# Spread weight rows and a straight scale product in a blockwise FP4 feed-forward kernel

## The reference

```python
def fp4_quant_dequant(x):            # BLOCK = 16, along the last dim
    xb = x.reshape(shape[:-1] + (shape[-1] // BLOCK, BLOCK))
    scale = jnp.max(jnp.abs(xb), axis=-1, keepdims=True) / 6.0
    scale = jnp.maximum(scale, jnp.float32(1e-12))
    xn = xb / scale
    idx = jnp.searchsorted(_MID, jnp.abs(xn))
    q = _GRID[idx] * jnp.sign(xn) * scale
    return q.reshape(shape)

def fp4_linear(x, w):
    return jnp.einsum('bsk,nk->bsn', fp4_quant_dequant(x), fp4_quant_dequant(w))

gate = fp4_linear(x, w_gate)
y = fp4_linear(x, w_up)
h = jax.nn.silu(gate) * y            # 1408 wide, quantised again inside the next line
return fp4_linear(h, w_down)
```

## Time and profile before

| | us |
|---|---|
| median of three runs | 1740.33 |
| lowest, highest | 1736.83, 1742.61 |
| the profiled execution | 1740.98 |
| its span in the profile | 1739.2 |
| TensorE busy | 1482.2 |
| ScalarE busy | 1347.2 |
| VectorE busy | 1169.9 |

### The profile page before, as it was taken

How to read it: one execution, slowest core, us unless ns; L and a number is a source line. 1 busy time by engine, 2 the same in 40 slices (tenths; PEclk the granted TensorE clock), 3 DMA queues, 4 the chain that set the end, 5 groups by cost and what they waited for, 6 DMA issues and landing times.

```text
span 1739.2 us, 23935 instructions
## 1 busy us (share of the span) xinstructions
PE 1482.2 (85%) x9752; PEld 651.5 (37%) x9752; DVE 1169.9 (67%) x2111; ACT 1347.2 (77%) x1391; POOL 2.7 (0%) x18
## 2 busy tenths in 40 slices
PE   6788888765888899889999999899999998689886
PEld 4234444311333333333333333333333334345442
DVE  4579999864475435467655555676555557999994
ACT  2798898899999999969999999699999992000000
POOL 0000000000000000000000000000000000000000
PEclk9999999888999999999999999999999999899997
DMA  3123332330011111211211111102211111122212
GB/s 129 37 62 75 74 75 63 76 73 15 13 24 35 35 35 24 36 35 16 55 36 36 36 36 35 36 13 59 35 36 36 35 36 36 37 54 62 58 41 51
DMA packets 180754, 77.88 MB, mean 45 GB/s; under 512 B 163851, under 2 KB 163851, under 8 KB 180645
## 3 DMA queue, kind: packets, MB, share of 16 engines
q1 hardware_dynamic: 177392, 74.99, 19.0%
q10 hardware_dynamic: 3253, 1.37, 0.3%
HBM read 27.85 MB, written 8.39 MB: 21 GB/s over the span
## 4 chain that ended last, share of the span: by engine, by line
ACT 56%; DVE 29%; PE 11%; issue 2%; ACTq 1%; DMA 1%; DVEq 0%; SPq 0%
ACT hring L438 54%; DVE work L703 4%; PE rho L548 3%; DVE work L714 2%; DVE work L715 2%; DVE sm L694 2%; ACT th L458 2%; DVE work L909 1%; DVE work L908 1%; DVE sm L697 1%; DVE work L713 1%; DVE work L712 1%; PE dn L623 1%; DVE work L716 1%; DVE work L717 1%
## 5 line engine op out<-in xcount | busy, mean ns | idle before, releaser
L438 ACT ACTIVATE hring<-featT,bias 128x1024 f32<-128x1024 f32 x1232 | 1293.0, 1140 | 80.9 <-PE rho L548 76.2
L548 PE MATMUL rho<-hring,wslide 128*32 128x512 f32 x4928 | 614.9, 623 | 136.7 <-ACT hring L438 136.7
L548 PEld LDWEIGHTS rho<-hring,wslide 128*32 128x32 f32 x4928 | 133.5, 112 | 499.9 <-ACT hring L438 271.7
L623 PE MATMUL dn<-wd_room,turned 128*128 128x512 f16 x1056 | 243.7, 383 | 13.4 <-DMA turned<-work 13.4
L908 DVE SCALAR_TENSOR_TENSOR work<-th,gu1g 128x352 f32<-128x352 f32 x64 | 33.3, 521 | 266.6 <-ACT th L458 265.9
L611 PE MATMUL gu0g<-wg,turned 128*128 128x352 f16 x768 | 134.6, 328 | 45.8 <-DVE work L909 29.0
L623 PEld LDWEIGHTS dn<-wd_room,turned 128*128 128x128 f16 x1056 | 99.2, 98 | 175.2 <-issue 54.6
L458 ACT ACTIVATE th<-gu0g 128x352 f32<-128x352 f32 x64 | 28.9, 451 | 171.5 <-PE gu0u L611 171.5
L611 PE MATMUL gu0u<-wu,turned 128*128 128x352 f16 x768 | 127.5, 317 | 0.0
L611 PE MATMUL gu1g<-wg,turned 128*128 128x352 f16 x768 | 126.2, 314 | 0.0
L611 PE MATMUL gu1u<-wu,turned 128*128 128x352 f16 x768 | 125.0, 313 | 0.0
(11 more groups left out here) (147 smaller groups left out, 1077.5 us busy)
## 6 DMA issues: line engine op xcount, KB each, us to landing
xt<-in_x SPq DMA_DIRECT2D x32, 256.0 KB, 2.8
out<-xt SPq DMA_DIRECT2D x32, 256.0 KB, 2.3
work<-in_x SPq DMA_DIRECT2D x10, 512.0 KB, 4.4
xt<-in_x SPq DMA_DIRECT2D x6, 512.0 KB, 3.9
xt<-in_L_ffn_w_gate SPq DMA_DIRECT2D x11, 256.0 KB, 2.6
xt<-in_L_ffn_w_up SPq DMA_DIRECT2D x11, 256.0 KB, 3.4
work<-in_L_ffn_w_down SPq DMA_DIRECT2D x2, 704.0 KB, 4.6
xt<-in_L_ffn_w_down SPq DMA_DIRECT2D x2, 704.0 KB, 4.6
```

Of the source, the lines that this page charges most:

```text
L438: act.activation(hring[:, s // 2, g, (s % 2) * 512:(s % 2) * 512 + rows], featT[:, e, ROW0[k]:ROW0[k] + rows], ACT.Tanh, bias=bias[:, e, b ...
L548: last = pe.matmul(rho[SLOTW * g:SLOTW * g + SLOTW, hf * 512:hf * 512 + 512], wslide[:, e, SLOTW - 1 - r:2 * SLOTW - 1 - r], hring[:, s // ...
L623: last = pe.matmul(dn[:, :], hqT[:, a, c, :], wd[:, bb, c, :], start=(c == 0 and i == 0), stop=(c == NC - 1 and i == 2))
```

## The change

`load_gu` issues 16 DMAs of 8 rows each instead of one of 128 rows, so that in each tile of 128 rows partition q * 8 + b holds row b * 16 + q. The transposed weights, and with them the columns of `h`, then lie in stored order from the start. VectorE's wait counts 16 times as much. `quantise` gets a flag, `spread`, set for `h` alone: its L694 reads the source at a step of 8 elements (over q inside, then over b), and its product with the reciprocal scale (before L703) reads and writes in straight order, with the reciprocal of block b repeated over q. The other three sources keep the old form.

```diff
             def load_gu(m, i):
-                sp.dma_start(xt[:, m, :], (gate_in, up_in)[m][i * P:(i + 1) * P, :]).then_inc(loaded_gu[m], 16)
+                rows = (gate_in, up_in)[m][i * P:(i + 1) * P, :].rearrange("(b q) d -> q b d", b=BPC)
+                for q in range(QB):
+                    sp.dma_start(xt[q * BPC:(q + 1) * BPC, m, :], rows[q]).then_inc(loaded_gu[m], 16)
...
-            def quantise(src, n, hi, lo, m, least, pre, read=None):
+            def quantise(src, n, hi, lo, m, least, pre, read=None, spread=False):
...
-                v = src.rearrange("p (m q) -> p m q", q=QB)
                 a, q = tA[:, 0:n], tq[:, 0:n]
-                step(dve.tensor_reduce(am, v, axis=AX_X, op=ALU.max, apply_absolute_value=True))
+                if spread:
+                    am_v, v = am.rearrange("p (i b) -> p i b", b=BPC), src.rearrange("p (i q b) -> p i b q", **natural)
+                else:
+                    am_v, v = am, src.rearrange("p (m q) -> p m q", q=QB)
+                step(dve.tensor_reduce(am_v, v, axis=AX_X, op=ALU.max, apply_absolute_value=True))
...
-                ins = tt(a.rearrange("p (i q b) -> p i b q", **natural),
-                         src.rearrange("p (i b q) -> p i b q", **natural),
-                         r.rearrange("p (i b) -> p i b", b=BPC).unsqueeze(3).broadcast_to([P, n // P, BPC, QB]), ALU.mult)
+                if spread:
+                    ins = tt(as_stored(a), as_stored(src), per_block(r), ALU.mult)
+                else:
+                    ins = tt(a.rearrange("p (i q b) -> p i b q", **natural),
+                             src.rearrange("p (i b q) -> p i b q", **natural),
+                             r.rearrange("p (i b) -> p i b", b=BPC).unsqueeze(3).broadcast_to([P, n // P, BPC, QB]),
+                             ALU.mult)
...
-                    dve.wait_ge(loaded_gu[m], 16 * (i + 1))
+                    dve.wait_ge(loaded_gu[m], 16 * QB * (i + 1))
...
-                signal(quantise(hbuf, INNER, hq[:, 0, :], hq[:, 1, :], hbuf, SCALE_MIN * lift, H_PRE / lift),
-                       hq_ready, t + 1)
+                signal(quantise(hbuf, INNER, hq[:, 0, :], hq[:, 1, :], hbuf, SCALE_MIN * lift, H_PRE / lift,
+                                spread=True), hq_ready, t + 1)
```

## The result

Twenty runs of each: the changed kernel has a median of 1745.7 us (1740.98 to 1747.67), the kernel before 1740.98 (1736.29 to 1745.39). The ratio is 1.0026, 95% interval [1.0016, 1.0036]: 0.26% slower, 4.7 us between the medians. The profiled execution took 1745.89 us, its span is 1744.0. One thing has to be known to read single profiles of this kernel: with nothing changed its times gather at two levels, near 1736.7 and near 1741.5 us, so that the span of one profile may be off by 5 us, and only the ratios with many runs settle a difference of this size.

A forecast was written before the change was run, and what follows sets the result against it. ScalarE was taken to bound the middle and VectorE the tail. Product -13.1, reduction +13.1 and loads 0 us sum to 0, so the forecast was 1740.3 us, from the median of 1740.33, range 1726 to 1750.

The forecast's parts named there:

- The product: VectorE's product of `h`, ten tail tiles and two softmax stages: falls to 1626 ns, saving 13.1 us of the chain.
- The reduction: VectorE's L694 over `h`: stepped reads cost what stepped writes cost, 2.70 to 2.76 us, giving the 13.1 us back.
- The rival of free reads: Reduction of `h`: stepped reads free or nearly so, it stays near 1.62 us, total 1727.2 us; chance 0.34.
- a read dearer than a write: Reduction of `h`: at twice the excess it takes 3.8 us, total 1753.4 us; chance 0.09.
- The loads in the weight stage: SyncE's sixteen issues a tile: 0.33 us each, 5.3 us in all, room 0.44 us an issue, cost nothing.
- the late queue: Weight stage: from 0.44 us an issue SyncE brings the next pair late; at 0.50 us, 1748.9 us; chance 0.10.
- The loads at the head: Ahead of the weight stage: 32 issues keep SyncE busy from some 4 to 15 to 20 us, cost nothing.
- The most likely case: Quantisation of `h`: reads cost what writes cost, own range 1735 to 1745.5 us; chance 0.47.

The follow-up runs named there:

- the run with 0.67 us an issue in that stage: Changed kernel with each tile loaded by 16 DMAs of 16 half rows at a partition step of 8: 1764.93 us, ratio 1.0138.
- the run of eight DMAs: Changed kernel with each tile loaded by 8 DMAs of 16 full rows at a partition step of 8: span 1741.5 us in one execution.

## Why the prediction was right and wrong

**The product**: right. 1625 ns against the 1626 forecast, by the straight row L714 of the earlier trace rows.

**The reduction**: right. 2.74 us on average and 2.69 in the tail against 2.70 to 2.76, by taking the price of a stepped read from the stepped write. The two together give back 19 ns a tile; the run with the quantisation alone has 0.9993, no difference. That the sum came to nothing was reasoned and not luck. The rival of free reads (0.34) is refuted, and so is that of a read dearer than a write at this step, 8 words: (2738 - 153) / 1408 = 1.84 ns an element against the write's 1.85. The 153 ns are what the straight 1620 leave over 1408 elements at 1.042, the slope between 1620 and the 686 ns of 512. At a step of 88 the read costs (3624 - 153) / 1408 = 2.47 ns an element. The stepped read of `h` costs 1.12 us more than the straight one (2738 - 1620), within the 1.08 to 1.14 taken from the row of the write.

**The loads in the weight stage**: right. 0.33 us an issue in most tiles and 0.40 at most, room to 0.44, no wait. The run with 0.67 us an issue in that stage has the late queue where it was forecast, and near its price: 3.66 us a pair by the formula, 3.2 on average in the trace. The changed kernel and the run of eight DMAs, with 4.9 to 6.5 us a tile, had no wait. Only the reason for such an issue time was another than the one given: sixteen issues in a string took 0.33 us each when they went to neighbouring partitions.

**The loads at the head**: wrong, and this is the whole miss. The step reads: "Ahead of the weight stage 32 issues keep SyncE busy from some 4 us to 15 to 20 us, and the load of pair 0 stands behind them", and "Cost nothing". It looked at one queue and asked who stands behind the issues in it. What another queue has to issue at the same time wasn't asked. ScalarE's mask loads are in such a queue, at 11.5 to 22.3 us, and they gate the first projection and with it the chain, which in the kernel before begins with ScalarE's DMA issues: of its first 26 us L396, the mask loads, holds 21.3%. That row was not among those that the step rested on. The cost measured: 4.76 us at the first projection (3.39 in the run with the loads alone), 0.26% in the time. The forecast of 1740.3 was 5.4 us too low, inside its range; 0.65 us of that lie in the kernel before, whose median over twenty executions is 1740.98 and not 1740.33. The most likely case was named for the right reasons in three of four parts, but the time did move. A second slip hid behind the first: a difference under 0.3% was called about as good as none, but with twenty executions of each the interval is 0.1% to either side, and 0.26% stands clear of it.

## What to carry to other kernels

A strided access that was moved from a write to a read wasn't removed here: product and reduction took 2762 + 1620 ns before and 1625 + 2738 after. Keeping two neighbouring words together removed it: 1626 + 1620. When a large DMA becomes many small ones, cost two things: the issues in its own queue against the slack of what stands behind them (sixteen at 0.33 to 0.40 us, under the room of 0.44, made no wait; sixteen at 0.62 to 0.70 made waits of 25.3 us in all), and the DMAs that other queues issue at that time (the four mask loads took 10.74 us instead of 5.63, and 7.97 with a quarter of the bytes), the head of the kernel above all, where in this case nothing hid the delay. The chain in order of time from zero is the view that shows whether a DMA issue gates the start.

## What the runs showed of the hardware that was not expected

A VectorE read of single float32 words costs 1.84 ns an element at a step of 8 words and 2.47 at a step of 88, against 1.04 straight; runs of two words, read at a step of 176 (1620 ns for 1408 columns) or written at a step of 176 (1626 ns), cost as much as straight ones, 1.04. SyncE takes 0.33 to 0.40 us to issue a DMA of 8 rows of 2 KB to neighbouring partitions, where one of 128 rows takes 0.33, and 0.62 to 0.77 us for 16 rows to every eighth partition, whether it moves 1 or 2 KB of each. For 16 rows to neighbouring partitions there is only the head, 0.46 to 0.51 us, against 0.63 to 0.65 there at the step, so not all of the doubling is the step's.
